# Retention block of a transformer layer on eight cores: a second PSUM bank for the Y accumulation, and six weight loads of some steps on another queue

## The reference, cut to what matters

```python
xn = layernorm(x)                                   # x: 32 x 2048 x 1024
# retention, 16 heads of width 64, gamma[h] between 0.9 and 0.999
q, k, v = heads(xn @ wq.T), heads(xn @ wk.T), heads(xn @ wv.T)
D = where(i >= j, gamma[h] ** (i - j), 0)
y = (q @ k.T * D) @ v                               # per head, over all 2048 positions
y = (y - mean(y)) * rsqrt(var(y) + eps)             # per sequence and head, over T and d
attn = (y * gn_w + gn_b) @ wo.T
# feed-forward, hidden 3072, weights int / 127
h = silu(xn @ wg.T) * (xn @ wu.T)
out = x + attn + h @ wd.T
```

## Time and profile before

| what | value |
|---|---|
| median of 2 runs | 4688.01 us (4428.22 and 4947.81) |
| the profiled execution | 4461.49 us |
| its span on the slowest core (4) | 4459.8 us |
| spans of the 8 cores | 4410.7 to 4459.8 us |
| PE busy on core 4 | 3691.8 us, 83% |
| DVE, ACT, POOL busy | 1371.9, 694.2, 343.3 us |

### The profile page before, as it was taken

How to read it: one execution, slowest core, us unless ns; L and a number is a source line. 1 busy time by engine, 2 the same in 40 slices (tenths; PEclk the granted TensorE clock), 3 DMA queues, 4 the chain that set the end, 5 groups by cost and what they waited for, 6 DMA issues and landing times.

```text
span 4459.8 us, 49312 instructions; the slowest of 8 cores (4410.7 to 4459.8 us)
## 1 busy us (share of the span) xinstructions
PE 3691.8 (83%) x17624; PEld 1652.5 (37%) x17624; DVE 1371.9 (31%) x2500; ACT 694.2 (16%) x1148; POOL 343.3 (8%) x476
## 2 busy tenths in 40 slices
PE   5209798998878888898968979799887988889898
PEld 2104343343433333343433434344333433334343
DVE  3101332424135141424134233242313415142412
ACT  2001121211012021111102112121101202121110
POOL 2110000000110000000020000000020000000002
PEclk9559798897988989897987979889898898989687
DMA  9995344343564334343573435344366343434255
GB/s 179 120 129 171 123 136 138 104 138 95 190 203 128 125 114 140 104 129 108 170 226 114 125 120 151 123 114 142 97 205 203 109 132 114 129 117 133 68 151 187
DMA packets 561037, 614.04 MB, mean 138 GB/s; under 512 B 15650, under 2 KB 425252, under 8 KB 559652
## 3 DMA queue, kind: packets, MB, share of 16 engines
q1 hardware_dynamic: 484260, 371.80, 28.4%
q0 software_dynamic: 42240, 155.21, 14.1%
q10 hardware_dynamic: 34304, 83.89, 5.8%
HBM read 560.51 MB, written 111.15 MB: 151 GB/s over the span
## 4 chain that ended last, share of the span: by engine, by line
PE 71%; DMA 10%; DVE 6%; issue 4%; another core or an unknown queue 4%; ACT 3%; POOL 1%; ACTq 0%; DVEq 0%; POOLq 0%; SPq 0%
PE pb L306 71%; DMA s_acc<-sb_xb 3%; DVE sb_ha L775 2%; DVE sb_xb L1061 2%; DMA sb_yb<-s_y 2%; ACT sb_yb L851 1%; DMA sb_wuw<-s_wu 1%; DVE sb_gn_acc L858 1%; DMA out<-sb_xb 1%; ACT sb_ha L735 1%; POOL sb_xn L554 1%; DMA sb_xb<-x 1%; PE pb L312 1%; DMA s_wu<-wuT 1%
## 5 line engine op out<-in xcount | busy, mean ns | idle before, releaser
L306 PE MATMUL pb<-sb_xn,sb_wuw 128*128 128x512 bf16 x3072 | 743.4, 386 | 100.8 <-DMA sb_wuw<-s_wu 100.8
L306 PE MATMUL pb<-sb_xn,sb_wgw 128*128 128x512 bf16 x3072 | 748.5, 388 | 82.5 <-DMA sb_wgw<-s_wg 82.5
L993 DVE SCALAR_TENSOR_TENSOR sb_ha<-pb,sb_silu 128x512 bf16<-128x512 f32 x384 | 265.7, 692 | 1125.4 <-PE pb L306 1099.1
L306 PE MATMUL pb<-sb_xn,sb_wset 128*128 128x512 bf16 x2048 | 479.8, 398 | 153.3 <-ACT sb_xn L469 145.2
L775 DVE TENSOR_TENSOR sb_ha<-pb,sb_mask 128x512 bf16<-128x512 f32 (+3 forms) x1024 | 418.3, 484 | 246.8 <-PE pb L306 246.7
L306 PEld LDWEIGHTS pb<-sb_xn,sb_wuw 128*128 128x128 bf16 x3072 | 304.8, 99 | 478.2 <-issue 143.6
L306 PEld LDWEIGHTS pb<-sb_xn,sb_wgw 128*128 128x128 bf16 x3072 | 304.0, 99 | 458.3 <-issue 128.4
L306 PE MATMUL pb<-sb_wdr,sb_ha 128*128 128x512 bf16 x2048 | 453.3, 383 | 0.0
L978 ACT ACTIVATE sb_silu<-pb 128x512 bf16<-128x512 f32 x384 | 228.8, 598 | 1161.1 <-PE pb L306 1157.9
L306 PE MATMUL pb<-sb_qt,sb_kt 64*128 64x512 bf16 (+3 forms) x1024 | 225.6, 412 | 219.7 <-DVE sb_ha L775 203.3
L306 PE MATMUL pb<-sb_wset,sb_xn 128*128 128x512 bf16 x1472 | 337.1, 392 | 42.7 <-POOL sb_xn L554 38.9
(11 more groups left out here) (82 smaller groups left out, 2043.6 us busy)
## 6 DMA issues: line engine op xcount, KB each, us to landing
sb_wgw<-s_wg SPq DMA_DIRECT2D x192, 512.0 KB, 4.2
sb_wuw<-s_wu SPq DMA_DIRECT2D x192, 512.0 KB, 5.6
sb_wdr<-s_wd SPq DMA_DIRECT2D x80, 512.0 KB, 11.0
sb_xb<-x ACTq DMA_DIRECT2D x64, 512.0 KB, 5.9
s_acc<-sb_xb POOLq DMA_DIRECT2D x16, 2048.0 KB, 10.2
sb_xb<-s_acc ACTq DMA_DIRECT2D x16, 2048.0 KB, 13.7
out<-sb_xb POOLq DMA_DIRECT2D x64, 512.0 KB, 6.7
sb_wset<-s_wq SPq DMA_DIRECT2D x15, 2048.0 KB, 8.9
```

What stands on the lines that cost most here:

```text
L306: e.matmul(o, l, r, start=s1, stop=s2),
L993: e.scalar_tensor_tensor(sb["ha"][:, 512 * fm:512 * (fm + 1)], b[:], INV127, sb["silu2"][:, 512 * (fm % 2): 512 * (fm % 2 + 1)], ALU.mult, ...
```

## The change

The first edit gives the Y chain of even pairs bank 7 and that of odd pairs bank 6, each with a token of its own in `y_free`, and hands both tokens to `bankfree` behind the loop. The second edit changes which queue loads the w_down quads: before, all quads of step 0 of every sequence were on the SP queue and the odd ones of the other steps on POOL's; now only step 0 of the first sequence is all on SP.

```diff
-            y_free = [bankfree[7]]
+            y_free = {7: bankfree[7], 6: bankfree[6]}
...
             def emit_ychain(pair, hh):
                 h = 2 * pair + hh
                 part = 64 * hh
+                yb_ = 7 - (pair % 2)
                 started = False
                 if sc > 0:
-                    mm([sbf_tok, qtev[pair], y_free[0]],
-                       pb[7][part:part + 64, 0:512],
+                    mm([sbf_tok, qtev[pair], y_free[yb_]],
+                       pb[yb_][part:part + 64, 0:512],
...
                     if not started:
-                        wy.append(y_free[0])
-                    y_tok = mm(wy, pb[7][part:part + 64, 128 * kc:512],
+                        wy.append(y_free[yb_])
+                    y_tok = mm(wy, pb[yb_][part:part + 64, 128 * kc:512],
...
+                ybk = 7 - (pair % 2)
...
-                    sb["yb"][:, 512 * p:512 * (p + 1)], pb[7][:], AF.Copy),
+                    sb["yb"][:, 512 * p:512 * (p + 1)], b[:], AF.Copy),
...
-                    sb["junk"][:, 512 * j:512 * (j + 1)], pb[7][:], AF.Square),
+                    sb["junk"][:, 512 * j:512 * (j + 1)], b[:], AF.Square),
                     waits=[junk_sq_free[jh]], inc="A")
-                y_free[0] = yev_last
+                y_free[ybk] = yev_last
...
-            bankfree[7] = y_free[0]
+            bankfree[7] = y_free[7]
+            bankfree[6] = y_free[6]
...
             def load_quad(j):
-                par_q = 0 if sc == 0 else wd_pair[0] % 2
+                par_q = 0 if (seq == 0 and sc == 0) else wd_pair[0] % 2
```

More of the change, by code:

```diff
@@ L848, in emit_program @@
                 y_tok = ydone[(pair, 1)]
+                ybk = 7 - (pair % 2)
                 col = 16 * sc + 2 * pair
                 jh = pair % 2
-                a_cp = E.op("scalar", lambda e, p=pair: e.activation(
-                    sb["yb"][:, 512 * p:512 * (p + 1)], pb[7][:], AF.Copy),
+                a_cp = E.op("scalar", lambda e, p=pair, b=pb[ybk]:
+                            e.activation(
+                    sb["yb"][:, 512 * p:512 * (p + 1)], b[:], AF.Copy),
                     waits=[y_tok, ysb_free, gn_prev], inc="A")
-                yev_last = E.op("scalar", lambda e, j=jh: e.activation(
-                    sb["junk"][:, 512 * j:512 * (j + 1)], pb[7][:], AF.Square),
+                yev_last = E.op("scalar", lambda e, j=jh, b=pb[ybk]:
+                                e.activation(
+                    sb["junk"][:, 512 * j:512 * (j + 1)], b[:], AF.Square),
                     waits=[junk_sq_free[jh]], inc="A")
-                y_free[0] = yev_last
+                y_free[ybk] = yev_last
                 E.op("vector", lambda e, p=pair, c=col: e.reduce_sum(
```

## The result

The changed kernel takes 1.0086 times the time of before, 95% interval 1.0074 to 1.0099: 0.9% slower, within the 2% named ahead, and clear of no change. Its median over 13 runs is 4470.4 us, that of before, over 10 runs now, 4461.96 us. Both medians contain runs in which one die had a lower clock; the ratio leaves them out. In the runs that it compares, before stands near 4428 us and the change near 4466 us, 38 us apart.

A forecast was written before the change was run, and what follows sets the result against it. PE, busy 83% of the span, was taken as the bound, with DVE's in-order queue holding the loop. 18.3 (wait) + 13 (clock) = 31.5 us on 4461.5 gave 4493 us; 4480 to 4506 had 66%, wider range 4445 to 4550.

The forecast's parts named there:

- the 2% named ahead: Whole kernel: 2% (89 us) taken as what a measurement can tell from no change; 89% chance of a result within it.
- the restart of the clock: Behind the new idle before the state: half clock for 4.0 us, 1.6 of it in the state, costing 1.2 a step.
- The new wait: Behind the loop, the first state matmul waits for pair 7's square in bank 6: 11 x 1.3 + 4 x 1.0 = 18.3 us.
- the group-norm steps: Four last steps of a sequence, group norm between state and FFN: 1.0 us later each, no clock cost.
- Step 0 of sequence 0: First step, which waits for staged weights: the state's shift disappears there, 0.
- The clock in the FFN: FFN of 11 steps starts partly at half rate after the new idle: 13 us, bounds 0 to 26.
- Edit 1, inside the retention loop: worth nothing: In the loop, bank 7's early release is hidden behind DVE's in-order queue: 0 for all 128 pairs.
- The queue edit: Step 0 of sequences 1 to 3, six w_down quads move from SyncE's queue to POOL's: cost 0.
- the loop gains: Rival: part of PE's 205.3 us wait on the DVE product belonged to bank 7; 4390 us, 4%.
- POOL is late: Rival: in step 0 POOL's w_down quads come late behind the wgw quad; 15 us more, 4508 us, 7%.
- The wait is all: Rival: the state's wait costs 18.3 us and the clock nothing; 4480 us, 15%.
- The lower grant in more steps: Rival: three more steps get the last step's lower granted clock, 25 us each; 4568 us, 6%.

The follow-up runs named there:

- the late sums: Kernel before with DVE's two sums of a pair emitted behind the next pair's head 0 masks: 0.9762 with one Y bank, 0.9751 with two exchanged banks.
- state_in_bank7: Kernel before, one Y bank, with the state accumulated in bank 7 too, so it waits for the square; no ratio, traced run 4476.38 us.
- gap_short: Changed kernel with the two banks exchanged and the first state matmul also waiting for ACT's copy, 0.8 us idle: ratio 1.0034 to before.

## Why the prediction was right or wrong

Two steps failed. The loop was put at 0 and lost 6 to 10 us by the gap, and the restart of the clock was taken at 4.0 us and cost 8.3 us in place of 13. The new wait, the largest term, was right in kind and 5.5 us too small.

- **The new wait: right in place and kind, too small.** 21.2 us in 16 waits of 1.33 were measured, where 21 were named, with the distance square to matmul 0.15 as taken. But a wait of 1.3 us moved the FFN by 1.55 (3.19 - 1.64), since the state's matmuls had begun before the modelled end of the Y chain, and now all 64 stand behind it, 1.86 us long. Nor was the state's 1.64 us the same "at any clock": before, four of the 11 steps had it in 1.32 to 1.39 us, at a granted clock of 0.65 to 0.70; now all have 0.50. So the mean delay of the 11 steps is 1.66 us. In the group-norm steps it was 1.4 us, not 1.0 (10.65 us from chain to FFN against 9.25). The term of 18.3 us measured 23.8.
- **Step 0 of sequence 0: right.** The wait is there (the sixteenth), and no loss shows in its FFN stage, which waits for the staged weights: 274.3 us against 276.5.
- **The clock in the FFN: right in kind, too large.** The grant fell from 0.97 to 0.83 in the first 4 us. The step that failed is "I take a restart of 4.0": the 11 stages lost 8.3 us, 0.75 each, not 1.2, so 1.5 us ran at half rate behind the state and not the 2.4 (4.0 - 1.6) taken. The four behind the group norm won 0.5 each, which I had at 0: the first 5.5 us of the one in sequence 0 had 0.50 before and 0.59 now.
- **"Edit 1, inside the retention loop: worth nothing": wrong by 6 to 10 us in the sum.** The reading of one pair stands: bank 7 was not what the pairs waited for, as the late sums show. But I looked for what two banks do to the loop and not for what the idle gap behind one loop does to the clock in the next ones, and `state_in_bank7` shows that the loss comes with the wait; by what path it reaches the later loops stays open. I also wrote that no row of PE's waits names the evictions of bank 7; the row of L735 holds one, 0.5 us at each loop's start, and the changed kernel keeps it only because it gives the first pair bank 7.
- **The queue edit: right**, 0.9998, with the down stage of step 0 at 41.69 us of busy PE against 41.57.
- **The rivals.** That the loop gains is out, and that POOL is late too. "The wait is all" is out by the FFN and by `gap_short`. The lower grant in more steps did not come with the change.
- **The sum and the number.** 31.5 us were forecast, about 38 measured. That they lie so near is luck in part, because the three errors (5.5 us short at the wait, 7 us too much at the FFN's clock, some 10 us missing in the loop) partly cancel. 4493 us itself is above the 4470.4 measured, since I built on an execution of before whose last step had the lower grant, 25 us by my own account; the 4428 us above plus the terms, 4428 + 31.5 = 4460, would have been nearer. The stretch with most of the chance, 4480 to 4506, missed the 4470.4; the wider range held it by the case it took in downwards, an execution whose last step has the usual clock. Against the 4688.01 us shown as the median of before, 4493 would even be a gain; that median was the middle of two unlike executions.

## What to carry to other kernels

A second buffer helps only if the wait for the first is the one that ends last: read what the waiting engine stands for, and how long the buffer had been free, before buying one. Where a buffer is borrowed from a later stage, look at which of the alternating users is the last, since that one is handed on with its readers' wait. And where an in-order engine does work nobody waits for (here two sums) ahead of work that the bottleneck waits for, moving it one place back was worth more here than a buffer: 2.4%, and 4.3% with one place more.

## What the runs showed of the hardware that I had not expected

- 0.8 us of idle time of TensorE ahead of a 1.9 us stretch of small matmuls brought the granted clock of the next stage's first 5 us from 1.00 to 0.81, and 2.2 us brought it to 0.68 (medians of 88 stages: 1.00, 0.80 and 0.66); the cost in the 11 FFN stages (10.9, 8.3 and 13.1 us for gaps of 0.8, 1.3 and 2.2 us) did not grow evenly with the gap.
- A loop with waits in it had different mean clocks for the same code, 0.59 or 0.55, some 10 us in 650, by what stands between the loops. Why a gap of 0.8 us left it alone and one of 1.3 us did not stays open.
